# Last block of a masked attention kernel: the context summed whole in PSUM, turned in squares of 32 and projected in blocks

## What is computed

```python
q = target_key @ W_target.T                       # 512 x 64
k = einsum('bld,ed->ble', item_keys, W_item)      # 512 x 200 x 64
v = einsum('bld,ed->ble', item_values, W_value)
scores = einsum('bd,bld->bl', q, k) / 8 + -1e8 * (1 - mask)
w = softmax(scores, axis=1)
out = einsum('bl,bld->bd', w, v)                  # 512 x 64
```

## Time and profile before

| | before |
|---|---|
| median of 3 runs | 134.1 us (133.74 to 134.16) |
| the profiled execution | 133.42 us |
| its span, first to last instruction | 131.5 us |
| busy: PE, DVE, ACT, POOL | 54%, 15%, 6%, 4% of the span |
| read from HBM | 53.07 MB, 404 GB/s over the span |
| chain that ended last | DMA 75%, PE 21%, the rest 4% |
| sizes of the loads | 6400 KB for each block of keys and of values, 7024 KB for the first |

### The profile page before, as it was taken

The page is one execution under the profiler, slowest core; times in us unless marked ns, Lnnn a source line. Parts: engine busy times, 40 slices in busy tenths (PEclk is TensorE's granted clock), DMA queues, the critical chain, the costliest instruction groups (busy, mean ns, idle before and its releaser), DMA issues.

```text
span 131.5 us, 1317 instructions
## 1 busy us (share of the span) xinstructions
PE 70.4 (54%) x536; PEld 21.5 (16%) x536; DVE 19.7 (15%) x55; ACT 7.8 (6%) x26; POOL 5.3 (4%) x18
## 2 busy tenths in 40 slices
PE   0000005995499203983279601985359976459671
PEld 0000002331122001330012100322111322111150
DVE  6000000103300500004200310003300040330240
ACT  3000001000200000011100000000300001020000
POOL 7400000000100000000000000000100000010000
PEclk9999999999869995599559995589658999976998
DMA  8699896999699979997999799979899899999921
GB/s 273 273 547 461 359 491 280 498 498 452 296 498 488 452 311 483 498 452 311 483 483 452 327 483 467 452 343 483 366 436 436 381 428 454 443 407 417 409 87 30
DMA packets 2562, 53.22 MB, mean 405 GB/s; under 512 B 768, under 2 KB 768, under 8 KB 1024
## 3 DMA queue, kind: packets, MB, share of 16 engines
q1 hardware_dynamic: 2016, 53.07, 94.2%
q10 hardware_dynamic: 544, 0.13, 0.5%
HBM read 53.07 MB, written 0.13 MB: 404 GB/s over the span
## 4 chain that ended last, share of the span: by engine, by line
DMA 75%; PE 21%; SPq 1%; issue 1%; DVE 0%; ACT 0%; DVEq 0%
DMA value<-values 75%; PE ps_context L466 8%; PE ps_context L475 4%; PE ps_context L483 4%; PE ps_context L469 2%; PE ps_late L506 2%; PE ps_small L494 0%; SPq L209 0%; SPq L188 0%; PE ps_small L513 0%; SPq L205 0%; ACT result L295 0%; DVE context_late L401 0%; DVE context_t L409 0%; DVEq L408 0%
## 5 line engine op out<-in xcount | busy, mean ns | idle before, releaser
L447 PE MATMUL ps_scores<-first_tile,sta_query 128*32 128x400 f32 x256 | 29.9, 621 | 17.8 <-DMA first_tile<-keys 17.3
L466 PE MATMUL ps_context<-value,sta_full 128*32 128x512 f32 x64 | 13.5, 996 | 7.9 <-DMA value<-values 7.9
L447 PEld LDWEIGHTS ps_scores<-first_tile,sta_query 128*32 128x32 f32 x256 | 9.2, 132 | 37.1 <-issue 19.5
L431 PE MATMUL ps_small<-first_tile 64*64 64x128 f32 x4 | 0.7, 443 | 20.3 <-DMA first_tile<-first 20.3
L352 DVE SCALAR_TENSOR_TENSOR second_biased<-ps_scores,in_pair,mask_bias 128x200 f32<-128x200 f32 x4 | 1.7, 426 | 43.9 <-PE ps_scores L447 43.9
L391 DVE TENSOR_TENSOR context_slots<-ps_context,in_octet 128x512 f32<-128x512 f32 x4 | 2.8, 692 | 34.6 <-PE ps_context L483 28.1
L475 PE MATMUL ps_context<-value,sta_half 128*32 128x512 f32 x64 | 7.7, 598 | 0.4 <-DMA value<-values 0.4
L246 POOL COPY half_twice<-expd 128x128 f32<-128x128 f32 x4 | 1.4, 345 | 109.9 <-ACT expd L270 109.9
L453 PE MATMUL ps_turn_full<-ident,expd 128*128 128x128 f32 x4 | 1.4, 350 | 8.2 <-ACT expd L270 8.2
L483 PE MATMUL ps_context<-value,sta_full 128*32 128x512 f32 x48 | 5.7, 592 | 0.0
L466 PEld LDWEIGHTS ps_context<-value,sta_full 128*32 128x32 f32 x64 | 2.4, 158 | 14.4 <-DMA value<-values 9.1
(11 more groups left out here) (48 smaller groups left out, 33.0 us busy)
## 6 DMA issues: line engine op xcount, KB each, us to landing
value<-values SPq DMA_DIRECT2D x3, 6400.0 KB, 22.9
first_tile<-keys SPq DMA_DIRECT2D x2, 6400.0 KB, 20.7
first_tile<-first SPq DMA_DIRECT2D x1, 7024.0 KB, 19.5
first_tile<-keys SPq DMA_DIRECT2D x1, 3200.0 KB, 13.6
first_tile<-keys SPq DMA_DIRECT2D x2, 1600.0 KB, 18.7
value<-values SPq DMA_DIRECT2D x1, 2304.0 KB, 12.5
value<-values SPq DMA_DIRECT2D x1, 2048.0 KB, 17.0
value<-values SPq DMA_DIRECT2D x1, 1280.0 KB, 19.5
```

What stands on the lines that cost most here:

```text
L447: last = nc.tensor.matmul(ps_scores[g * GU:(g + 1) * GU, 0:QB], window(sta_query, g, k), key[:, c:c + QB], start=k == 0, stop=k == QUADS - 1)
L466: nc.tensor.matmul(ps_context[g * GU:(g + 1) * GU, :], window(sta_full, g, k), value[:, c:c + OB], start=k == 0, stop=False)
```

## The change

In the last block the octet work is as before, but for the order: the second half's octets now stand ahead of the halves in all blocks, and the last block's halves are in the loop too, behind a branch that waits for their piece. The late pairs k = 0 to 6 go to `ps_late` as before. Then:

- The context is not added by VectorE. `add_whole` puts it into a 128 x 64 region of PSUM, `ps_whole`, as a product of the 128 x 128 identity and `context`. It is the first of the sum and stands between k = 4 and k = 5, behind the wait for the piece of 512 KB and a wait for `context`.
- VectorE masks the sum of k = 0 to 6 by parity (`keep_own_late`, 128 x 128, with a 128 x 2 `parity`), out to `own_late`.
- The last pair of each group is weighed singly (`weigh_singles`): eight matmuls of 64 columns that add straight into the rows of `ps_whole`, four for each of the two users, with a new stationary tile, `late_single`.
- Two more identity products add the two halves of `own_late`.
- VectorE turns `ps_whole` in squares of 32 x 32 (`turn_whole`), out to `turned`. TensorE projects it with eight matmuls of 32 x 32 weights and 64 columns, each on the tile of its own rows. For this a copy of W_value with its 32-row parts exchanged is made at the start (`swap_value_weights`, four copies on ScalarE).
- At the start, `w_both` comes from one matmul of 64 rows and two copies in place of two matmuls and one copy. `own_parity` and its four memsets go; `late_single` gets a memset on GpSimd, `parity` a small reduce on VectorE.

The diff, with declarations of tiles and semaphores left out:

```diff
-        ps_w_both = ps_small[:, 256:256 + 2 * D]
-        ps_context_t = ps_small[:, 0:P]
+        ps_w_both = ps_small[0:D, 256:256 + 2 * D]
+        ps_context_t = ps_small[0:D, 0:P]
         ps_project = ps_small[:, P:P + D]
+        ps_whole = ps_query[0][:, 0:D]
...
             nc.gpsimd.memset(late_full[:], 0.0).then_inc(s_late_zero, 1)
+            nc.gpsimd.memset(late_single[:], 0.0).then_inc(s_late_zero, 1)
...
         def _(act):
-            act.wait_ge(s_both, 2)
-            nc.scalar.mul(w_both[:], ps_w_both, float(D) ** -0.5).then_inc(s_both_copied, 1)
+            act.wait_ge(s_both, 1)
+            for h in range(2):
+                nc.scalar.mul(w_both[h * D:(h + 1) * D, :], ps_w_both, float(D) ** -0.5).then_inc(s_both_copied, 1)
...
             def place_odd_queries(n):
...
             def place_late_full():
-                act.wait_ge(s_late_zero, 1)
+                act.wait_ge(s_late_zero, 2)
                 nc.scalar.copy(
...
                     ps_full_t.rearrange("p (g s i e) -> p g s i e", g=GRP, s=NT, e=2)[:, :, 1]).then_inc(s_late_full, 1)
+                nc.scalar.copy(late_single[:, :, GU - 2::GU + 1],
+                               ps_full_t.rearrange("p (g u) -> p g u", g=GRP)[:, :, GU - 2:GU]).then_inc(s_late_single, 1)
+            def swap_value_weights():
+                for q in range(P // QUARTER):
+                    source = q + 1 - 2 * (q % 2)
+                    nc.scalar.copy(w_value_other[q * QUARTER:(q + 1) * QUARTER, :],
+                                   w_value_twice[source * QUARTER:(source + 1) * QUARTER, :]).then_inc(s_other, 1)
...
             def copy_context_t(n):
...
                     act.wait_ge(s_project, n)
-                nc.scalar.copy(context_t[0:D, :], ps_context_t[0:D, :]).then_inc(s_context_t_copied, ROUND)
+                nc.scalar.copy(context_t[:], ps_context_t).then_inc(s_context_t_copied, ROUND)
...
             def finish(n):
...
             place_odd_queries(0)
+            swap_value_weights()
             for n in range(NBLK):
...
         def _(dve):
             nc.vector.memset(sta_query[:], 0.0).then_inc(s_query_zero, 1)
-            for e in range(2):
-                nc.vector.memset(own_parity[e * D:(e + 1) * D, :, e], 1.0).then_inc(s_parity, 1)
-                nc.vector.memset(own_parity[e * D:(e + 1) * D, :, 1 - e], 0.0).then_inc(s_parity, 1)
             dve.wait_ge(s_ident, 1)
...
             nc.vector.tensor_reduce(in_pair[:], place_in_quad[:].rearrange("p (b e) -> p b e", e=2), AX_X, ALU.add) \
+                .then_inc(s_places, 1)
+            nc.vector.tensor_reduce(parity[:], place_in_quad[:].rearrange("p (b e) -> p e b", e=2), AX_X, ALU.add) \
                 .then_inc(s_places, 1)
...
             def place_even_queries(n):
...
-            def add_late():
-                dve.wait_ge(s_context, ROUND * NBLK)
+            def keep_own_late():
+                dve.wait_ge(s_places, 4)
                 dve.wait_ge(s_late_done, 1)
-                nc.vector.tensor_tensor(context_late[:], ps_late[:, 0:VB].rearrange("p (e d) -> p e d", e=2),
-                                        context[:].unsqueeze(1).to_broadcast([P, 2, D]), ALU.add) \
-                    .then_inc(s_context_late, 1)
-            def keep_own_late():
-                dve.wait_ge(s_parity, 4)
-                dve.wait_ge(s_project, NBLK - 1)
-                dve.wait_ge(s_context_t, NBLK)
-                nc.vector.tensor_tensor(context_t[:], ps_context_t, own_parity[:].rearrange("p i e -> p (i e)"),
-                                        ALU.mult).then_inc(s_context_t_copied, ROUND)
+                nc.vector.tensor_tensor(own_late[:], ps_late[:, 0:VB].rearrange("p (e d) -> p e d", e=2),
+                                        parity[:].unsqueeze(2).to_broadcast([P, 2, D]), ALU.mult).then_inc(s_own_late, 1)
+            def turn_whole():
+                dve.wait_ge(s_whole, 1)
+                nc.vector.transpose(turned[:], ps_whole).then_inc(s_turned, 1)
...
                 take_context(n)
-            add_late()
             keep_own_late()
+            turn_whole()
...
         def _(pe):
             pe.wait_ge(s_key, 16)
-            for h in range(2):
-                rows = slice(h * D, (h + 1) * D)
-                nc.tensor.matmul(ps_w_both[rows, :], w_target[rows, :],
-                                 w_item[rows, :].unsqueeze(1).to_broadcast([D, 2, D]),
-                                 start=True, stop=True).then_inc(s_both, 1)
-            pe.wait_ge(s_both_copied, 1)
+            nc.tensor.matmul(ps_w_both, w_target[0:D, :], w_item[0:D, :].unsqueeze(1).to_broadcast([D, 2, D]),
+                             start=True, stop=True).then_inc(s_both, 1)
+            pe.wait_ge(s_both_copied, 2)
             for h in range(2):
...
-            def weigh_halves(last_of_block):
+            def weigh_halves():
                 for s in range(NT):
...
                         last = nc.tensor.matmul(ps_context[g * GU:(g + 1) * GU, :], window(sta_half, g, s),
-                                                value[:, c:c + OB], start=False, stop=last_of_block and s == NT - 1)
-                return last
+                                                value[:, c:c + OB], start=False, stop=s == NT - 1)
+                last.then_inc(s_value_used, 1)
...
             def weigh_second():
...
                         c = B_FULL + (k * GRP + g) * OB
-                        last = nc.tensor.matmul(ps_context[g * GU:(g + 1) * GU, :], window(sta_full, g, OCTS_T + k),
-                                                value[:, c:c + OB], start=False, stop=k == OCTS_T - 1)
-                last.then_inc(s_value_used, 1)
+                        nc.tensor.matmul(ps_context[g * GU:(g + 1) * GU, :], window(sta_full, g, OCTS_T + k),
+                                         value[:, c:c + OB], start=False, stop=False)
...
             def turn_context(done):
...
                 pe.wait_ge(s_context, done)
-                nc.tensor.transpose(ps_context_t[0:D, :], context[:], ident[:]).then_inc(s_context_t, 1)
-            def project(done, rows):
+                nc.tensor.transpose(ps_context_t, context[:], ident[:]).then_inc(s_context_t, 1)
+            def project(done):
                 pe.wait_ge(s_context_t_copied, done)
-                nc.tensor.matmul(ps_project, context_t[0:rows, :], w_value_twice[0:rows, :], start=True, stop=True) \
+                nc.tensor.matmul(ps_project, context_t[:], w_value_twice[0:D, :], start=True, stop=True) \
                     .then_inc(s_project, 1)
...
+            def add_whole(rows, ready, count, start=False, stop=False):
+                pe.wait_ge(ready, count)
+                return nc.tensor.matmul(ps_whole, ident[:], rows, start=start, stop=stop)
             def weigh_late():
-                pe.wait_ge(s_value_piece[0], 16)
-                weigh_halves(True).then_inc(s_value_used, 1)
                 pe.wait_ge(s_late_full, 1)
-                for k in range(PAIRS_T):
+                for k in range(PAIRS_T - 1):
                     if k in CUTS:
                         pe.wait_ge(s_value_piece[CUTS.index(k) + 1], 16)
+                    if k == CUTS[1]:
+                        add_whole(context[:], s_context, ROUND * NBLK, start=True)
                     for g in range(GRP):
...
                         last = nc.tensor.matmul(ps_late[g * GU:(g + 1) * GU, 0:VB], late_full[:, g, k * GU:(k + 1) * GU],
-                                                value[:, c:c + VB], start=k == 0, stop=k == PAIRS_T - 1)
+                                                value[:, c:c + VB], start=k == 0, stop=k == PAIRS_T - 2)
                 last.then_inc(s_late_done, 1)
...
-            def turn_context_late():
-                pe.wait_ge(s_context_late, 1)
+            def weigh_singles():
+                pe.wait_ge(s_late_single, 1)
+                pe.wait_ge(s_value_piece[len(CUTS) - 1], 16)
+                for e in range(2):
+                    for g in range(GRP):
+                        c = B_FULL + ((PAIRS_T - 1) * GRP + g) * VB + e * D
+                        nc.tensor.matmul(ps_whole[g * GU:(g + 1) * GU, :], late_single[:, g, e * GU:(e + 1) * GU],
+                                         value[:, c:c + D], start=False, stop=False)
+            def project_turned():
                 pe.wait_ge(s_result, NBLK - 1)
-                nc.tensor.transpose(ps_context_t, context_late[:].rearrange("p e d -> p (e d)"), ident[:]) \
-                    .then_inc(s_context_t, 1)
+                pe.wait_ge(s_other, P // QUARTER)
+                pe.wait_ge(s_turned, 1)
+                for b in range(D // QUARTER):
+                    for q in range(P // QUARTER):
+                        rows = slice(q * QUARTER, (q + 1) * QUARTER)
+                        weights = w_value_twice if b == q % 2 else w_value_other
```

(15 more changed lines are left out.)

17 lines of the change are left out of this document (12 added, 5 removed).

## The result

| | before | changed | ratio, 95% interval |
|---|---|---|---|
| median of the comparison | 133.44 us (22 runs) | 134.23 us (22 runs) | 1.0052 (1.0037 to 1.0067) |
| the same, second comparison | 133.54 us (35 runs) | 134.07 us (12 runs) | 1.0050 (1.0027 to 1.0073) |
| profiled execution, span | 133.42, 131.5 us | 134.54, 132.6 us | |

The change makes the kernel slower by 0.5% (about 0.7 us; 0.8 and 0.5 us by the medians). The first median of the kernel before is lower than the one of three runs shown ahead (134.1), so it is the ratio that is to be held against the forecast: +0.55 us on 134.1 was +0.4%.

A forecast was written before the change was run, and what follows sets the result against it. DMA transfers were taken to bound the kernel until 125.27 us, leaving only the tail to count. Its steps summed to a projection end of 129.84 against 129.29: +0.55 on 134.1, so 134.6 us, range 133.9 to 135.2.

The forecast's parts named there:

- What costs nothing: Start and loop: added copies, memsets, reduce, new order and branch are covered by transfers or waits, so add nothing.
- The context product: Tail, TensorE between k=4 and k=5: the product and shape changes make k=5 start 0.47 us later.
- The new wait for it in front of the context product adds nothing: Last block: VectorE's reduce of the context ends at 126.12, 0.41 us before k=5 starts, so waiting costs nothing.
- Own late: Tail: VectorE masks the k=0 to 6 sum in 0.29 us; usable at 128.13, later than the singles free TensorE.
- Passes of the singles: Tail, TensorE during the mask: four passes of four tiles, 0.11 us each (0.055 if half), not setting the time.
- Two identity products: Tail, TensorE after the mask: four passes taking 0.65 us, between 0.54 and 0.75.
- VectorE's transpose: Tail: turning 128x64 out of PSUM takes 0.24 us, with hand-overs of 0.14 before and 0.06 after.
- Projection: Tail, TensorE: eight products, four tiles at a time, are four passes taking 0.62 us, between 0.43 and 0.65.
- A: Tail: with the last two landings over 1.10 us apart, late work is covered; −0.4 to +0.1 us, 134.0; chance 0.17.
- B: Tail: 32*32 tiles writing one PSUM bank take turns, 16 passes for four; 0.4 to 1.3 us more, 135.5; chance 0.10.
- C: Tail before k=5: context product costs next to nothing as the next weights load meanwhile; +0.08 us, 134.2; chance 0.17.

The follow-up runs named there:

- the short reduce: Changed kernel, but in the last block VectorE sums only 2 of the 8 context slots, for timing only; 134.06 us, ratio 1.0046.
- the early half: Changed kernel with pairs k=5 to 7 weighed singly, the rest added and turned early, both turned tiles projected into one sum; 133.35 us, ratio 0.9979.

## Why the prediction was right, and where its steps were not

The forecast was +0.55 us, slower; the ratios say +0.5%, about 0.7 us (0.5 to 0.8 by the medians). Step by step, against the second profile of the changed kernel, whose context was in time:

- **What costs nothing**, start and loop: right. The old tail with the rest of the change runs as before.
- **The context product**: +0.47 forecast. k=5 starts 0.11 before the landing, in the kernel before 0.59 before it (126.53, 127.12): 0.48. Right, and enough by itself for the loss: taken out of there, the loss goes; put back alone, it comes. What stays unexplained is that the wait put back alone brings a loss as large, and both together no more.
- **"The new wait for it in front of the context product adds nothing"**: this step failed. It used one execution's 0.41 us of slack (126.12 to 126.53). That slack hangs on where TensorE's low clock falls in the last block. The reduce ended between 126.1 and 126.5 in ten profiles, at 127.01, 127.26 and 127.92 in three. The kernel before used the context at 127.70 and had 1.58 us of slack; the change cut that by three quarters. It cost 0.54 us in one profile of the changed kernel and nothing in the other.
- **Own late**: right. k=5 to VectorE's mask 0.78 (126.94 to 127.72), usable at 128.07, TensorE waiting 0.26 for it.
- **Passes of the singles**: 16 records of 64 columns in 0.41, so a pass of four takes about 0.055, the lower end, not 0.11. It is off the path, as said.
- **Two identity products**: 0.66 for 0.65. Right.
- **VectorE's transpose**: 0.25 for 0.24. The hand-over to it is 0.03 and the one behind it 0.15 (128.73 to 128.76, 129.01 to 129.16), for 0.14 and 0.06; the sum, 0.18, is 0.02 less.
- **Projection**: the term that was mis-sized. 0.42 (129.16 to 129.58) for 0.62, below even the lower end of 0.43: its four passes start within 0.21, where 0.35 was summed.

By the profile the tail is then 0.38 longer (2.59 for 2.21) where +0.55 was summed: 0.2 too much for the projection. What the medians have above that, 0.15 to 0.4 us, is of the size of the forgotten wait, but the run with the short reduce does not confirm that split. That the forecast came out near the measured value is in part luck: a term too dear stood in for one left out.

**The rivals.** A (late work covered) did not come. It needed the last two landings over 1.10 us apart; in the changed kernel's second profile the two pieces were issued 0.48 apart and took 20.4 and 20.6 us, so they landed about 0.7 apart. B (the 32*32 tiles take turns) is refuted: all 16 passes of the projection are done in 0.42 (129.16 to 129.58), and 16 turns of even 0.055 would take 0.88. The four tiles of the first pass start within 0.02 us. The Trainium skill's rule that different row tiles cannot access one bank at once (page TensorEngine Tiling (Array Packing), section Gotcha 1: PSUM Pressure) is not borne out here: four row tiles, each with PSUM rows of its own, wrote one bank side by side. C (the context product costs next to nothing) is refuted by the rows: k=5 starts 0.37 after the product in both kernels that have it in time. What the prediction did not list was the wait by a late clock.

## What to carry to other kernels

An operation put in front of work that is already late can cost its whole length, however small: a product of 64 columns through the full array, with the array's shape changed for it and back, held the tiles behind it up by 0.48 us here, and the tail became 0.31 us longer. Behind the last work the same operation cost less, some 0.2 us by the rows, and the time was that of the kernel before. A new wait has to be checked against executions in which the clock is low at another place, and not against the slack of one profile: ask what the slack hangs on. And a tail that is cut by 0.6 us on the engines need not show in the time: look at the last store's landing too, which here took 1.0 us longer in the profile of that kernel.

## What the runs showed of the hardware

- Sixteen passes of f32 matmuls with 32*32 weights and 64 columns, four tiles abreast, start within 0.21 us (129.16 to 129.37) and take 0.42 in all, each with its own weight load. Four tiles of 128*32 with 64 columns: 16 passes in 0.41.
- VectorE turned 128x64 f32 in squares of 32 in 0.24 to 0.25 us, out of PSUM or out of SBUF alike; one, directly behind another, took 0.21.
- TensorE's low clock lay at 117 to 120 in one execution, over all of 113.7 to 122 in another of nearly the same program, and over the halves at 122.5 in a third. VectorE's context was ready at 126.12, 127.26 and 127.92 in these. No profile of the old tail has a late context; its slack was 1.58 us.
- A store of 32 KB took 1.5 us to land in eleven profiles and 2.5 and 2.6 in two, those of the kernels with the early half and two stores. No run told why.
